# Experts of a two-layer AdaLN network: all tokens through all experts, or pairs sorted into 39 blocks

## The chip, the cores and the metric

The kernel runs on one core of one Trainium2 chip. The metric is the device time of one execution in microseconds. The core's engines are TensorE (PE, matrix products; PEld is its weight load), VectorE (DVE), ScalarE (ACT), GpSimd (POOL) and SyncE (SP, which issues transfers). Each runs its own program in order and waits for others by semaphores.

## What is computed

The reference has two layers; each adds a feed-forward result to `x` (8 sequences of 256 tokens, 512 channels). The first layer's condition is a chain of 256 oscillator steps, the second's is an attention with 16 heads. The change touches the last part only, the experts of the second layer:

```python
scores = einsum('btd,de->bte', x, router_w)
w, idx = top_k(softmax(scores), 2)
w = w / sum(w)
act = silu(x @ gate_proj[e]) * (x @ up_proj[e])     # 512 -> 256, for e in idx
out = sum over e in idx of w_e * (act @ down_proj[e])   # 256 -> 512
x = x + out
```

There are 2048 tokens, 8 experts and 2 chosen experts per token, so 4096 pairs of token and expert count; the reference is written over all 16384 and multiplies the others by zero.

## The kernel before

`build` runs three stages, each a block of its own: `oscillator_and_ffn`, `attention` and `experts`. The attention leaves its output y transposed in SBUF, channels on the partitions, as two 16-bit halves (`YH` the rounded value, `YL` the rest), and during it POOL prepares the gate and up weights of all experts as two halves in `WU`, scaled by 64. Every product is taken as high x high, high x low and low x high.

`experts` (from line 1187) first computes the router's scores with 192 small products (line 1294) into `dp[0]`; `route` on VectorE finds the two largest (lines 1346 and 1349), the two weights, and with 32 small operations (lines 1359 and 1360) a table `comb` of weights by token and expert. Meanwhile POOL scales and splits the down weights (lines 1245 to 1252).

Then the work runs over 4 groups of 512 tokens, and in a group over the 8 experts. For each expert and each half `fc` of its 256 hidden channels, `gate_up` (line 1270) takes 12 gate and 12 up products with the weights stationary and 512 tokens moving; ScalarE takes a tanh (line 1316), VectorE makes the hidden values and their two halves in four operations (lines 1368 to 1376). `down` (line 1284) takes 6 products for each of 4 tiles of 128 tokens, hidden values stationary, and VectorE's `fold` (line 1384) adds the result, times the token's weight for this expert, onto `acc`, which was loaded with the tokens of x (line 1233) and is stored at the end of the group (line 1236). TensorE's order per expert is: first half's gate and up, the previous expert's down, second half's gate and up.

Of the kernel before, what the change touches and what calls it, by code (L numbers as in the profile page):

```python
# [15 lines left out]
ALU = mybir.AluOpType  # L16
# [19 lines left out]
REP = 4  # L36

# [1142 lines left out]
def experts(nc, x1_dram, router, w_down, iota, WU, WD, YH, YL, out):  # L1180
    with ExitStack() as ctx:
# [6 lines left out]
        def psum(name):  # L1188
            return ctx.enter_context(nc.psum_tensor("moe_" + name, [P, 512], F32))

        TT = 4
        NG = B // 2
        NT = NG * TT
        dst = sb("dst", [P, HC, D])
        rst = sb("rst", [P, DC, E])
        rw = sb("rw", [P, 2, DC, E], F16)
        io = sb("io", [P, E])
# [8 lines left out]
        c1 = sb("c1", [P, NT, E])  # L1206
        comb = sb("comb", [P, NT * E])
        th = sb("th", [P, 2, 512])
        ga = sb("ga", [P, 512])
        hf = sb("hf", [P, 512])  # L1210
        hid = sb("hid", [P, FC, 2, 512], F16)
        acc = sb("acc", [P, TT, D])
        gp = [psum("gp0"), psum("gp1")]
        up = [psum("up0"), psum("up1")]
        dp = [psum(f"dp{i}") for i in range(TT)]
        FIRST = 2 * FC
        in_d = [sem("in_d0"), sem("in_d1")]
        in_r, d_scaled, d_hi, d_lo, r_hi, r_lo = (sem("in_r"), sem("d_scaled"), sem("d_hi"), sem("d_lo"), sem("r_hi"),
                                                  sem("r_lo"))
        sc_mm, dif_ok, ex_ok, comb_ok, own = sem("sc_mm"), sem("dif_ok"), sem("ex_ok"), sem("comb_ok"), sem("own_dve")  # L1220
        g_mm, u_mm, th_ok, hid_ok, d_mm, folded = sem("g_mm"), sem("u_mm"), sem("th_ok"), sem("hid_ok"), sem("d_mm"), sem("folded")
        acc_in, stored, ffn_own, halt = sem("acc_in"), sem("stored"), sem("ffn_own"), sem("halt3")
        block = ctx.enter_context(nc.Block())

        @block.sync
        def _(sp):
            sp.dma_start(rst[:], router).then_inc(in_r, 16)
            sp.dma_start(io[:], iota).then_inc(in_r, 16)
            sp.dma_start(dst[:, 0:FIRST], w_down[:, 0:FIRST]).then_inc(in_d[0], 16)
            sp.dma_start(dst[:, FIRST:HC], w_down[:, FIRST:HC]).then_inc(in_d[1], 16)  # L1230
            with sp.Fori(0, NG) as g:
                for tt in range(TT):
                    sp.dma_start(acc[:, tt], x1_dram[g * 2 + tt // 2][:, tt % 2]).then_inc(acc_in, 16)
                for tt in range(TT):
                    sp.wait_ge(folded, (g * E + E) * TT + tt + 1)
                    sp.dma_start(out[g * 2 + tt // 2][:, tt % 2], acc[:, tt]).then_inc(stored, 16)
                sp.wait_ge(stored, (g * TT + TT) * 16)
                sp.sem_inc(halt, 1)

        @block.gpsimd  # L1240
        def _(pool):
            def split_down(n):

                w = dst[:, bass.ds(n, 1)]
                pool.tensor_copy(WD[:, bass.ds(n, 1), 0], w).then_inc(d_hi, 1)
                pool.wait_ge(d_hi, n + 1)
                pool.sem_inc(halt, 1)
                pool.tensor_tensor(WD[:, bass.ds(n, 1), 1], w, WD[:, bass.ds(n, 1), 0], ALU.subtract).then_inc(d_lo, 1)

            for k, (first, last) in enumerate(((0, FIRST), (FIRST, HC))):  # L1250
                pool.wait_ge(in_d[k], 16)
                pool.tensor_scalar_mul(dst[:, first:last], dst[:, first:last], WS).then_inc(d_scaled, 1)
                pool.wait_ge(d_scaled, k + 1)
                pool.sem_inc(halt, 1)
                with pool.Fori(first, last) as n:
                    split_down(n)

        @block.tensor
        def _(pe):
            pe.wait_ge(r_lo, 1)  # L1260

            def gate_up(g, e, fc):

                n = (g * E + e) * FC + fc
                pe.wait_ge(hid_ok, n - FC + 1 + FC)
                for which, ps, done in ((0, gp[fc], g_mm), (1, up[fc], u_mm)):
                    k = 0
                    for wp, Yp in ((0, YH), (1, YH), (0, YL)):
                        for qt in range(DC):
                            last = pe.matmul(ps[:, :], WU[:, e * FC + fc, which, wp, qt, :],  # L1270
                                             Yp[:, bass.ds(g * 2, 2), qt, :], start=(k == 0), stop=(k == 3 * DC - 1))
                            k += 1
                    last.then_inc(done, 1)

            def down(g, e):
                pe.wait_ge(hid_ok, (g * E + e) * FC + FC + FC)
                pe.wait_ge(d_lo, e * FC + FC)
                for tt in range(TT):

                    pe.wait_ge(folded, (g * E + e) * TT + tt + 1)  # L1280
                    k = 0
                    for fc in range(FC):
                        for hp, wp in ((0, 0), (0, 1), (1, 0)):
                            last = pe.matmul(dp[tt][:, :], hid[:, fc, hp, tt * P:(tt + 1) * P], WD[:, e * FC + fc, wp, :],  # L1284
                                             start=(k == 0), stop=(k == 3 * FC - 1))
                            k += 1
                    last.then_inc(d_mm, 1)


            for tt in range(NT):  # L1290
                k = 0
                for wp, Yp in ((0, YH), (1, YH), (0, YL)):
                    for qt in range(DC):
                        last = pe.matmul(dp[0][:, tt * E:(tt + 1) * E], Yp[:, tt // 2, qt, (tt % 2) * P:(tt % 2 + 1) * P],  # L1294
                                         rw[:, wp, qt, :], start=(k == 0), stop=(k == 3 * DC - 1))
                        k += 1
            last.then_inc(sc_mm, 1)
            with pe.Fori(0, NG) as g:
                gate_up(g, 0, 0)
                gate_up(g, 0, 1)  # L1300
                with pe.Fori(1, E) as e:
                    gate_up(g, e, 0)
                    down(g, e - 1)
                    gate_up(g, e, 1)
                down(g, E - 1)

        @block.scalar
        def _(act):
            act.wait_ge(in_r, 32)
            act.activation(rw[:, 0].rearrange("p k e -> p (k e)"), rst[:].rearrange("p k e -> p (k e)"), ACT.Copy, scale=WS).then_inc(r_hi, 1)  # L1310

            def gate_tanh(g, e, fc):
                n = (g * E + e) * FC + fc
                act.wait_ge(g_mm, n + 1)
                act.wait_ge(hid_ok, n + 1)
                act.activation(th[:, fc], gp[fc][:, :], ACT.Tanh, scale=0.5 / WS).then_inc(th_ok, 1)
# [3 lines left out]
            with act.Fori(0, NG) as g:  # L1320
                with act.Fori(0, E) as e:
                    for fc in range(FC):
                        gate_tanh(g, e, fc)

        @block.vector
        def _(dve):
            dve.wait_ge(in_r, 32)
# [3 lines left out]
            dve.sem_inc(hid_ok, FC)  # L1331

            def route():

                k = [0]

                def step(ins):
                    ins.then_inc(own, 1)
                    k[0] += 1
                    dve.wait_ge(own, k[0])  # L1340

                dve.wait_ge(sc_mm, 1)
                step(dve.tensor_copy(sc[:].rearrange("p t e -> p (t e)"), dp[0][:, 0:NT * E]))
                dve.sem_inc(folded, TT)
                for tt in range(NT):
                    last = dve.max(top[:, tt], sc[:, tt])  # L1346
                step(last)
                for tt in range(NT):
                    last = dve.max_index(idx[:, tt], top[:, tt], sc[:, tt])  # L1349
                step(last)  # L1350
                dve.tensor_tensor(dif[:], top[:, :, 1], top[:, :, 0], ALU.subtract).then_inc(dif_ok, 1)
                step(dve.tensor_copy(idf[:], idx[:, :, 0:2]))
                dve.wait_ge(ex_ok, 1)

                step(dve.tensor_scalar(den[:], ex[:], WS, WS, ALU.mult, ALU.add))  # L1355
                step(dve.reciprocal(wt[:, 0], den[:]))
                step(dve.tensor_tensor(wt[:, 1], wt[:, 0], ex[:], ALU.mult))
                for tt in range(NT):
# [111 lines left out]
```

## Time and profile before

| | us |
|---|---|
| median of 3 runs | 3412.77 (3406.76 to 3414.52) |
| span of the profiled execution, first to last instruction | 3403.6 |
| its experts stage, from the attention's last slice to the end | 554.6 |

The runs lie 3 to 11 us above the span, which leaves out what happens ahead of the first and behind the last instruction; no time from outside is listed for the profiled execution itself. The profile gives for each engine the time in which it executes; TensorE's granted clock stands beside it in tenths or as a share of 2.4 GHz.

### The profile page before, as it was taken

The page shows a single profiled execution, that of the slowest core. Times are in us where ns is not written, and L with a number is a line of the kernel's source. Part 1 is how long each engine was busy: PE and PEld are TensorE (multiplying, and loading weights), DVE is VectorE, ACT ScalarE, POOL GpSimd, SP SyncE. Part 2 cuts the span into 40 slices and gives each one's busy share as a digit, 9 for nine tenths or more (in the row PEclk, how much of TensorE's full clock was granted, in tenths as well). Part 3 has the DMA queues.
Part 4 walks back from the last instruction along what each step waited for, and adds up shares of the span by engine and source line. Part 5 has one row for each costly group of instructions (what it writes and reads, how often), then busy time and mean ns, then how long its engine had stood idle before and what let it go on. Part 6 is the DMA issues. An engine that isn't in the chain of part 4 may idle for free. (4 is left out here: it accounts for less than half of the span.)

```text
span 3403.6 us, 128007 instructions
## 1 busy us (share of the span) xinstructions
PE 2702.1 (79%) x41104; PEld 1867.1 (55%) x41104; DVE 2621.4 (77%) x12682; ACT 1136.9 (33%) x3078; POOL 1361.7 (40%) x4206
## 2 busy tenths in 40 slices
PE   3377777777777777777777779988889995999999
PEld 2256566666555555555555546655556664444444
DVE  8888888888888888888888457788887877544444
ACT  2332222222222222222222247777776763000000
POOL 6745555555555555555555223323333325100000
PEclk9989988899999999999999875578885557999999
DMA  4100000000000000000000240111111011000000
GB/s 175 39 5 9 4 10 10 10 4 9 10 10 4 9 10 10 4 10 10 10 4 10 100 137 23 32 42 38 34 42 37 18 30 63 0 25 12 12 25 12
DMA packets 44052, 90.18 MB, mean 26 GB/s; under 512 B 7168, under 2 KB 23808, under 8 KB 41600
## 3 DMA queue, kind: packets, MB, share of 16 engines
q1 hardware_dynamic: 36336, 63.11, 5.8%
q10 hardware_dynamic: 4752, 10.49, 0.8%
q0 software_dynamic: 2304, 8.39, 0.8%
q8 instruction: 340, 5.57, 0.7%
q14 instruction: 320, 2.62, 0.3%
HBM read 65.18 MB, written 16.78 MB: 24 GB/s over the span
## 5 line engine op out<-in xcount | busy, mean ns | idle before, releaser
L225 PE MATMUL rest<-Tl,CW 128*128 128x32 f16 x16384 | 583.6, 179 | 489.6 <-DVE Tl L474 488.4
L225 PEld LDWEIGHTS rest<-Tl,CW 128*128 128x128 f16 x16384 | 489.8, 97 | 702.6 <-DVE Tl L474 693.5
L1060 PE MATMUL Tps<-idS,Pr 128*128 128x128 f32 x2048 | 425.7, 376 | 47.3 <-ACT Pr L1110 39.4
L1140 DVE CUSTOM_DVE_ANT_0 negL<-Lps,negC 128x512 f32<-128x512 f32 x512 | 342.2, 686 | 151.7 <-PE Lps L1050 134.8
L1060 PEld LDWEIGHTS Tps<-idS,Pr 128*128 128x128 f32 x2048 | 338.5, 194 | 164.4 <-DVE PT L1160 99.1
L644 POOL TENSOR_TENSOR G<-X,Dr 128x32 f32<-128x32 f32 x1024 | 268.6, 262 | 373.0 <-DVE X L479 299.0
L344 ACT ACTIVATE Tf<-X 128x32 f32<-128x32 f32 x768 | 176.1, 229 | 659.5 <-DVE X L554 658.2
L1117 ACT ACTIVATE PT<-Tps 128x512 f16<-128x512 f32 x512 | 300.1, 595 | 221.1 <-PE Tps L1060 220.5
L1110 ACT ACTIVATE Pr<-negL,nM 128x512 f32<-128x512 f32 x512 | 362.2, 720 | 20.3 <-DVE nM L1140 16.9
L1160 DVE TENSOR_TENSOR PT<-Tps,PT 128x512 f16<-128x512 f32 x512 | 348.2, 681 | 14.7 <-ACT PT L1117 10.0
L214 PE MATMUL main<-Th,CW 128*128 128x32 f16 x8224 | 250.9, 178 | 57.7 <-ACT Th L349 17.8
L1050 PE MATMUL Lps<-KR,QR 64*128 64x512 f16 x512 | 247.4, 519 | 42.1 <-issue 21.6
L214 PEld LDWEIGHTS main<-Th,CW 128*128 128x128 f16 x8224 | 225.0, 97 | 83.3 <-ACT Th L349 73.0
L648 POOL TENSOR_SCALAR gm<-X 128x32 f32<-128x32 f32 x768 | 233.7, 304 | 64.6
L1384 DVE SCALAR_TENSOR_TENSOR moe_acc<-moe_dp,moe_comb,moe_acc 128x512 f32<-128x512 f32 x128 | 96.1, 750 | 194.5 <-PE moe_dp L1284 194.5
L245 PE MATMUL gate<-Xa,WU 128*128 128x128 f16 x3072 | 236.3, 232 | 1.4 <-DVE Xa L562 1.4
L466 DVE TENSOR_TENSOR square<-X 128x32 f32<-128x32 f32 x1024 | 207.7, 203 | 32.6 <-DVE X L554 7.7
L245 PE MATMUL up<-Xa,WU 128*128 128x128 f16 x3072 | 229.9, 229 | 0.0
L1008 POOL TENSOR_TENSOR yf<-yn 128x64 f32<-128x64 f32 x128 | 40.9, 320 | 451.3 <-DVE yn L1154 451.3
L462 DVE SCALAR_TENSOR_TENSOR net<-main,G 128x32 f32<-128x32 f32 x768 | 142.7, 186 | 96.6 <-POOL G L644 90.8
L255 PE MATMUL acc_ps<-WD,hid 128*128 128x512 f16 x768 | 209.9, 382 | 0.6 <-ACT hid L358 0.6
L470 DVE SCALAR_TENSOR_TENSOR cube<-square,X 128x32 f32<-128x32 f32 x1024 | 204.3, 200 | 2.6 <-DVE lin L482 2.5
(135 smaller groups left out, 5056.4 us busy)
## 6 DMA issues: line engine op xcount, KB each, us to landing
stage<-w_up SPq DMA_DIRECT2D x8, 1024.0 KB, 4.8
qk<-qkp ACTq DMA_DIRECT2D x32, 256.0 KB, 2.4
QR<-qk SPq DMA_DIRECT2D x128, 64.0 KB, 2.2
KR<-qk SPq DMA_DIRECT2D x128, 64.0 KB, 2.4
wstage<-moe_up POOLq DMA_DIRECT2D x16, 512.0 KB, 6.3
W2m<-w_down SPq DMA_DIRECT2D x1, 4096.0 KB, 13.5
stage<-x_tb SPq DMA_DIRECT2D x16, 256.0 KB, 2.7
x<-stage SPq DMA_DIRECT2D x16, 256.0 KB, 2.6
```

The lines of the kernel that those rows point to most:

```text
L214: last = pe.matmul(main[:, m], CW[:, wp, k, m * P:(m + 1) * P], Th[:, par, k:k + 1, :].to_broadcast([P, REP, B]), start=(wp == 1 and m == ...
L225: last = pe.matmul(rest[:, m], CW[:, 0, k, m * P:(m + 1) * P], Tl[:, k:k + 1, :].to_broadcast([P, REP, B]), start=(m == 0 and k == 0), sto ...
L245: ins = pe.matmul(out[:, 0:P], WU[:, hc, which, wp, k, :], Xa[:, xp, k, :], start=(n == 0), stop=(n == 3 * DC - 1))
L255: ins = pe.matmul(acc_ps[:, :], hid[:, hp, :], WD[:, hc, wp, :], start=False, stop=False, skip_group_check=True)
L644: pool.tensor_tensor(G[:, s % 2, :], n, Dr[:, t, :], ALU.add).then_inc(drive_ready, 1)
L648: own.then_wait(pool.tensor_scalar_mul(gm[:], n, -EPS * a * BETA))
L1050: pe.matmul(Lps[qt % 2][:, :], QR[base:base + 64, h // 2, qt * P:(qt + 1) * P], KR[base:base + 64, h // 2, :], start=True, stop=True).then ...
L1060: last = pe.transpose(Tps[kc][:, qt * P:(qt + 1) * P], Pr[:, h % 2, qt, kc * P:(kc + 1) * P], idS[:])
L1110: act.activation(Pr[:, h % 2, qt, :], negL[:, qt, :], ACT.Exp, bias=nM[:, h % 4, qt:qt + 1], scale=-1.0).then_inc(s_exp, 1)
L1117: act.activation(PT[:, h % 2, 0, kc, :], Tps[kc][:, :], ACT.Copy).then_inc(s_hi, 1)
L1140: dve.tensor_tensor_reduce(out=negL[:, qt, :], in0=Lps[qt % 2][:, :], in1=negC[:], scale=1.0, scalar=3.0e38, op0=ALU.add, op1=ALU.min, acc ...
L1160: dve.tensor_tensor(PT[:, h % 2, 1, kc, :], Tps[kc][:, :], PT[:, h % 2, 0, kc, :], ALU.subtract).then_inc(s_lo, 1)
```

## The change

The pairs of token and expert are sorted on chip. Each expert has a region of 2048 + 128 rows in a buffer `xd` in device memory. A token tile's slot in the region comes from prefix sums over the one-hot mask (triangular and all-ones matrices in `moe_const`, products in `positions`). TensorE turns y back to tokens on the partitions (`token_rows`), ScalarE and four times VectorE copy it out as rows of 1024 16-bit values (high and low half), and POOL writes the rows with 32 indirect transfers, two for each of 16 tiles. SP pads each region's end with 128 zero rows, and 7 spare blocks. VectorE computes a table that gives, for each of 39 blocks of 128 rows (4096 / 128 + 7), the expert (`own_e`) and the first row (`own_r`).

The 39 blocks are written out one by one. For each, SP reads the row number out of SBUF into a register (`value_load`) and loads the block; TensorE turns it (8 transposes), takes 12 products with the tokens stationary and 512 columns of gate and up weights moving, turns the hidden values (4 transposes) and takes 6 down products; ScalarE copies the result out and SP stores it to `od`. At the end POOL gathers the two results of each token with 32 indirect transfers from `od` (into the space of `WU`), and VectorE adds them to x with the two weights. The split of the down weights is ScalarE's and VectorE's now. The buffers of the blocks lie in the space of `YH` and `YL`.

```diff
+            sp.wait_ge(padded, 16 * (E + SPARE))
+            sp.wait_ge(table_ok, 2)
+            sp.wait_ge(sent, 2 * NT * 16)
+
+            def load(i):
+                row = sp.value_load(own_r[0:1, i:i + 1], min_val=0, max_val=E * REGION + (SPARE - 1) * P)
+                if i >= NX:
+                    sp.wait_ge(t_mm, i - NX + 1)
+                sp.dma_start(xblk[:, i % NX], xd[bass.ds(row, P), :]).then_inc(x_in[i % NX], 16)
+
+            for i in range(NX - 1):
+                load(i)
+            sp.wait_ge(d_lo, HC)
+            for t in range(NT):
+                sp.dma_start(acc[:, t], x1_dram[t // 2][:, t % 2]).then_inc(acc_in, 16)
+            for i in range(NBLK):
+                if i + NX - 1 < NBLK:
+                    load(i + NX - 1)
+                sp.wait_ge(d_ok, i + 1)
+                sp.dma_start(od[i * P:(i + 1) * P, :], outs[:, i % NX]).then_inc(o_out[i % NX], 16)
+            for t in range(NT):
+                sp.wait_ge(sum2, t + 1)
+                sp.dma_start(out[t // 2][:, t % 2], acc[:, t]).then_inc(stored, 16)
...
         @block.gpsimd
         def _(pool):
...
+            pool.wait_ge(slot_ok, 1)
+            for t in range(NT):
+                wait_rows(pool, t)
+                for k in range(2):
+                    pool.indirect_dma_start(xd[:, :], bass.IndirectOffsetOnAxis(slot[:, k, t:t + 1], 0), rows[:, t], None).then_inc(sent, 16)
+            pool.wait_ge(home_ok, 1)
+            for n in range(NX):
+                pool.wait_ge(o_out[n], 16 * len(range(n, NBLK, NX)))
+            for t in range(NT):
+                for k in range(2):
+                    pool.indirect_dma_start(got[:, t, k], None, od[:, :],
+                                            bass.IndirectOffsetOnAxis(home[:, k, t:t + 1], 0)).then_inc(got_in[t // 2], 16)
...
         @block.tensor
         def _(pe):
...
+            def turn(i):
+                if i >= 2:
+                    pe.wait_ge(t_ok, i - 1)
+                pe.wait_ge(x_in[i % NX], 16 * (i // NX + 1))
+                for n in range(2 * DC):
+                    last = pe.transpose(tp[i % 2][:, n * P:(n + 1) * P], xblk[:, i % NX, n * P:(n + 1) * P], mats[:, 0])
+                last.then_inc(t_mm, 1)
+
+            def gate_up(i):
+                e = pe.value_load(own_e[0:1, i:i + 1], min_val=0, max_val=E - 1)
+                pe.wait_ge(t_ok, i + 1)
...
+                for q in range(DC):
+                    for xp, wp in ((0, 0), (0, 1), (1, 0)):
+                        last = pe.matmul(gu[i % 2][:, :, :, :], yt[:, i % 2, xp, q, :], WU[:, bass.ds(e * FC, FC), :, wp, q, :],
+                                         start=(n == 0), stop=(n == 3 * DC - 1))
...
+            turn(0)
+            turn(1)
+            e = gate_up(0)
+            pe.wait_ge(d_lo, HC)
+            for i in range(NBLK):
+                if i + 1 < NBLK:
+                    nxt = gate_up(i + 1)
+                turn_hidden(i)
+                if i + 2 < NBLK:
+                    turn(i + 2)
+                down(i, e)
+                e = nxt
...
         @block.scalar
         def _(act):
...
+            turned(0)
+            turned(1)
+            gate_tanh(0)
+            high(0)
+            for i in range(NBLK):
+                if i + 2 < NBLK:
+                    turned(i + 2)
+                if i + 1 < NBLK:
+                    gate_tanh(i + 1)
+                    high(i + 1)
+                out_copy(i)
...
         @block.vector
         def _(dve):
...
+            gated(0)
+            for i in range(NBLK):
+                hidden_turned(i)
+                if i + 1 < NBLK:
+                    gated(i + 1)
+            dve.wait_ge(acc_in, NT * 16)
+            for t in range(NT):
+                dve.wait_ge(got_in[t // 2], 16 * 4)
+                dve.scalar_tensor_tensor(acc[:, t], got[:, t, 0], wt[:, 0, t:t + 1], acc[:, t], ALU.mult, ALU.add).then_inc(sum1, 1)
+                dve.wait_ge(sum1, t + 1)
+                dve.scalar_tensor_tensor(acc[:, t], got[:, t, 1], wt[:, 1, t:t + 1], acc[:, t], ALU.mult, ALU.add).then_inc(sum2, 1)
```

Left out above: ScalarE's `turned` copies a turned block out of PSUM (128x1024), `gate_tanh` and `high` handle 128x256, `out_copy` copies the result of 128x512 and gives the signal `d_ok`. VectorE's `gated` makes the hidden values (two products of 128x256, then the low half), `hidden_turned` copies the turned hidden values out of PSUM.

## Rows read from the trace of the kernel before

**Rows 1.** Page, first line; timeline, POOL, end of the attention (start us, us).

```profile
span 3403.6 us, 128007 instructions
...
2848.71 0.30 POOL L1014 TENSOR_TENSOR YL<-yf,YH 128x64 f16<-128x64 f32 x1 [0.18 <-POOL YH L1011]
```

**Rows 2.** Busy time in the experts: stretch, us, engines (instructions), clock, DMA share, GB/s.

```profile
core 0: us, PE busy (x) PEld busy (x) DVE busy (x) ACT busy (x) POOL busy (x), PEclk, DMA share, GB/s
...
2898.00:3400.00 502.00, 493.17 (x2256) 221.57 (x2254) 247.11 (x379) 37.02 (x62) 11.75 (x13) 0.99 0.04 14
```

**Rows 3.** Page, part 4: the chain that ended last, shares by engine.

```profile
PE 15%; DVE 1%; issue 0%; DMA 0%; DVEq 0%; ACT 0%; SPq 0%
```

**Rows 4.** Timeline of the experts: two sweeps of down products; the last sum.

```profile
2967.40 5.34 PE L1284 MATMUL moe_dp<-WE,moe_hid 128*128 x24
...
2982.94 2.32 PE L1284 MATMUL moe_dp<-WE,moe_hid 128*128 x10
...
3400.20 0.75 DVE L1384 SCALAR_TENSOR_TENSOR moe_acc<-moe_dp,moe_comb,moe_acc 128x512 f32<-128x512 f32 x1 [0.54 <-PE moe_dp L1284]
```

**Rows 5.** Chain in order of time, way into the experts: start us, us, what.

```profile
2853.99 5.30 PE moe_dp L1294 x192
...
2860.97 2.28 DVE moe_idx L1349 x17
...
2865.56 0.29 DVE moe_c L1359
...
2893.02 0.65 DVE moe_comb L1362
...
2893.90 0.70 DVE moe_ga L1368
```

**Rows 6.** Timeline of the first layer: twelve products of 128 columns.

```profile
1501.52 0.83 PE L245 MATMUL gate<-Xa,WU 128*128 128x128 f16 x12
```

**Rows 7.** Timeline of the experts: products after a pause.

```profile
2897.59 3.59 PE L1270 MATMUL moe_gp<-YH,WU 128*128 x8 [26.71 <-DVE moe_hid L1376]
...
2902.65 1.89 PE L1270 MATMUL moe_up<-YH,WU 128*128 x8
...
3392.99 7.04 PE L1284 MATMUL moe_dp<-WE,moe_hid 128*128 128x512 f16 x24 [2.21 <-DVE moe_hid L1376]
```

**Rows 8.** Busy time in the attention, a stretch of 4 us (columns as rows 2).

```profile
2036.00:2040.00 4.00, 4.00 (x44) 2.79 (x43) 2.62 (x7) 3.62 (x7) 0.00 (x0) 0.50 0.03 6
```

**Rows 9.** Groups by shape, whole kernel: busy us, mean ns, idle before.

```profile
L1154 DVE TENSOR_TENSOR yn<-Ops,ri 128x128 f32<-128x128 f32 x128 | 35.9, 280 | 0.1
...
L869 DVE TENSOR_TENSOR V<-vp,V 128x256 f32 x32 | 12.1, 420 | 1.2 <-ACT V L831 0.3
L831 ACT ACTIVATE V<-vp 128x256 f32 x32 | 11.6, 390 | 2.7 <-PE vp L807 2.1
...
L436 DVE SCALAR_TENSOR_TENSOR WU<-stage,WU 128x512 f16<-128x512 f32 x32 | 21.8, 682 | 0.0
...
L825 ACT ACTIVATE qkp<-qp 128x512 f16<-128x512 f32 x16 | 8.8, 595 | 23.6 <-PE qp L798 19.5 <-issue 4.1
```

**Rows 10.** Instructions on tiles wstage and moe_acc: ns min/median/max, first, last start.

```profile
L984 POOL DMA_DIRECT2D wstage<-moe_up x16: 527/578/762, 2015.6 to 2740.7; - x16
L989 POOL TENSOR_SCALAR wstage<-wstage x16: 2765/2768/2770, 2042.7 to 2794.0; 128x1024 f32<-128x1024 f32 x16
...
L1233 SPq MOVE moe_acc<-x x16: 29/29/38, 2853.2 to 3276.9; - x16
L1233 SPq DMA_DIRECT2D moe_acc<-x x16: 332/346/570, 2853.2 to 3276.9; - x16
```

**Rows 11.** DMA view of 2851 to 2875, 40 slices of 0.6 us.

```profile
GB/s 0 3 29 167 55 341 410 437 587 410 655 246 410 601 205 492 492 287 532 492 174 331 304 403 413 256 55 38 7 0 0 0 0 0 0 0 0 0 0 0
DMA packets 1154, 5.30 MB, mean 221 GB/s; under 512 B 384, under 2 KB 384, under 8 KB 896
```

**Rows 12.** DMA issues of the kernel: count, KB each, median us to landing.

```profile
stage<-x_tb SPq DMA_DIRECT2D x16, 256.0 KB, 2.7
...
out<-moe_acc SPq DMA_DIRECT2D x16, 256.0 KB, 2.0
...
moe_rst<-router SPq DMA_DIRECT2D x1, 16.0 KB, 1.6
```

**Rows 13.** Waits of the whole kernel: us in total, times, longest us.

```profile
DVE X L457 <- issue: 39.1, 13, 3.3
```

More of the change, by code:

```diff
@@ L1177, in _, with experts @@
             all_heads(dve, step)
-def experts(nc, x1_dram, router, w_down, iota, WU, WD, YH, YL, out):
+def experts(nc, x1_dram, xd, od, router, w_down, const, WU, WE, YH, YL, out):
     with ExitStack() as ctx:
@@ L1220, in experts @@
[L1220 to L1223 removed]
+        oh = sb("oh", [P, 2, NT, E])
+        mask = sb("mask", [P, NT, E], F16)
+        place = sb("place", [P, NT, E])
@@ new lines, in experts @@
+        prod = sb("prod", [P, 2, NT, E])
+        slotf = sb("slotf", [P, 2, NT])
+        slot = sb("slot", [P, 2, NT], U32)
+        home = sb("home", [P, 2, NT], U32)
+        shift = sb("shift", [P, E])
+        cnt = sb("cnt", [P, E])
+        over = sb("over", [P, E, NT])
+        nb = sb("nb", [P, E])
+        part = sb("part", [P, E, E])
+        ends = sb("ends", [P, E])
+        past = sb("past", [P, NBLK, E])
+        gone = sb("gone", [P, NBLK, E])
+        who = sb("who", [P, NBLK])
@@ L1227, in _ @@
             sp.dma_start(rst[:], router).then_inc(in_r, 16)
[L1228 to L1238, printed above, removed]
+            sp.dma_start(cst[:], const).then_inc(in_c, 16)
@@ L1240, in _ @@
+            sp.wait_ge(stored, NT * 16)
         @block.gpsimd
         def _(pool):
[L1242 to L1246, printed above, removed]
-                pool.sem_inc(halt, 1)
[L1248 to L1256, printed above, removed]
+            pool.memset(blank[:], 0.0).then_inc(blank_ok, 1)
@@ L1275, in down @@
[L1275 to L1287, printed above, removed]
@@ L1296, in _, with token_rows @@
                         k += 1
             last.then_inc(sc_mm, 1)
[L1298 to L1305, printed above, removed]
+            pe.wait_ge(mats_ok, 1)
+            def token_rows(t):
+                if t >= 2:
+                    wait_rows(pe, t - 2)
+                for w, Yp in ((0, YH), (1, YL)):
+                    for q in range(DC):
+                        last = pe.transpose(tp[t % 2][:, (w * DC + q) * P:(w * DC + q + 1) * P],
+                                            Yp[:, t // 2, q, (t % 2) * P:(t % 2 + 1) * P], mats[:, 0])
+                last.then_inc(rows_mm, 1)
@@ new lines, in step, with flat @@
+            def step(ins):
+                ins.then_inc(own, 1)
+                k[0] += 1
+                dve.wait_ge(own, k[0])
+            def flat(x):
+                return x.rearrange("p t e -> p (t e)")
+            dve.wait_ge(in_c, 16)
+            dve.wait_ge(sc_mm, 1)
+            step(dve.tensor_copy(flat(sc[:]), rt[:, 0:P]))
+            for t in range(NT):
+                last = dve.max(top[:, t], sc[:, t])
+            step(last)
+            for t in range(NT):
+                last = dve.max_index(idx[:, t], top[:, t], sc[:, t])
@@ new lines, in _ @@
+            step(last)
+            step(dve.tensor_copy(idf[:], idx[:, :, 0:2]))
+            for w in range(2):
+                last = dve.tensor_tensor(oh[:, w], idf[:, :, w:w + 1].to_broadcast([P, NT, E]),
+                                         iota_e.unsqueeze(1).to_broadcast([P, NT, E]), ALU.is_equal)
+            step(last)
+            dve.tensor_tensor(mask[:], oh[:, 0], oh[:, 1], ALU.add).then_inc(mask_ok, 1)
+            dve.tensor_tensor(dif[:], top[:, :, 1], top[:, :, 0], ALU.subtract).then_inc(dif_ok, 1)
```

331 lines of the change are left out of this document (225 added, 106 removed).

## The prediction

> **What bounds the kernel now.** I read the page's parts 1 to 4 first, then the stretch of the experts alone, because that is the only stage that the change touches. The stage begins when POOL has written the last slice of the attention's output, at 2849.0 us, and ends with the span at 3403.6 [rows 1]: 554.6 us. In the stretch from 2898 to 3400, TensorE is busy 493 of 502 us at a granted clock of 0.99 (2.4 GHz), VectorE about half of it, ScalarE 7% and POOL 2% [rows 2]; the chain that ended last is TensorE's gate, up and down products [rows 3]. The timeline shows the pace: from one sweep of down products to the next are 15.54 us [rows 4], and a sweep (one expert, 512 tokens) has 72 products of 512 columns, so 0.216 us each. 32 sweeps are 497 us. The rest is the way in: scores at 2854, routing on VectorE until the first hidden block at 2893.9 [rows 5]. So here TensorE's columns are the bound, and most of them are wasted: every token goes through 8 experts and needs 2.
>
> **What the change removes.** 39 blocks of 18 products of 512 columns are 702 products instead of 2304. With 12 transposes a block TensorE has 18 x 0.216 + 12 x 0.06 = 4.6 us of work per block at the high clock (0.06 is the pace of the 128-column products [rows 6]). At the low clock a 512-column product takes 0.43 (eight in 3.59 us [rows 7]) and a block 18 x 0.43 + 12 x 0.11 = 9.0. That is 180 to 351 us. TensorE is no longer the natural bound; what comes in its place is a chain of waits, and I price that.
>
> **Way in.** Scores and the top-two search are as before, to 2863.2 [rows 5]. Then one-hot and mask, four operations of 128x128 at about 0.28 [rows 9]: 2864.4. Meanwhile TensorE turns eight token tiles and ScalarE copies them out, 128x1024 each. From 128x256 in 0.39 and 128x512 in 0.595 [rows 9] such a copy takes 0.595 + 512 x 0.0008 = 1.0 us; eight with hand-offs end near 2868.5. The prefix sums (32 small products) follow in TensorE's order, then five small VectorE operations: slots known at **2872**. The removed loop of 32 VectorE operations (2865.6 to 2893) pays for this part.
>
> **Scatter.** POOL now issues 32 indirect transfers, one after the other. The trace has no indirect transfer. The nearest row is POOL's plain one of 512 KB, 0.58 us of POOL [rows 10], and it computes no address per row; that is the lower end. Upwards I bound by four times that, 2.3, since each of 128 rows needs its index read and an address written; I take 1.1, twice the plain one. The Trainium skill (DMA: Bandwidth & Descriptors, Anatomy of one DMA) calls the cost of writing descriptors small; by it 0.58 would stand, data would bind, and the sum would be 16 us less. 32 x 1.1 = 35 us. The data is no harder limit: 8.4 MB plus 2.1 MB of padding at 0.35 MB/us (5.3 MB in 25 busy slices of 0.6 us [rows 11]) are 30 us. With a landing of 2.5 the last row is in memory at **2910**. Hidden beside it: the rest of the table, the other eight tiles, and the split of the down weights, moved from POOL to ScalarE and VectorE (16 x 0.6 and 16 x 0.68 us [rows 9], about 2888 to 2900). The data's 30 us cover them; without that cover they would cost at most 11.
>
> **First block.** SP looks up a row number in SBUF and loads block 0. The look-up (value_load) is not in the trace either. Lower end: a register MOVE, 0.03 [rows 10]; upper end: the shortest transfer, 1.6 [rows 12]. I take 1.0, nearer the upper end since it too must fetch from SBUF. The Trainium skill (DMA: Bandwidth & Descriptors, Latency and other measured facts) gives about 0.6 as the floor of such a load; by it each round below would be 0.4 shorter, the sum 14 us less. Then 0.48 to issue and 2.5 to land [rows 10, 12]. TensorE is at the low clock by then. Turn, copy, 12 products, hidden values, the products of block 1, and only then the turn of block 2, whose load stands on SP behind 16 issues of the x1 tiles (16 x 0.49 = 7.8): block 0's output is copied at about **2934**.
>
> **The rounds.** This is the term that decides. SP's order in the loop is: load block i+2, wait for block i's output, store it. So the load of block i+2 is queued behind the wait for block i-1's output (`d_ok`), and ScalarE's order is copy of turned block i+2, tanh of i+1, high half of i+1, output copy of i. Hence a closed chain from output i-1 to output i:
> - SP wakes 0.1, issues the store 0.48 (0.35 and a MOVE, with gaps [rows 10]), looks up the row 1.0, load to landing 2.5 (256 KB tiles took 2.0 to 2.7 [rows 12]; behind a store): 4.1.
> - TensorE sees it 0.15; eight transposes 1.0 at the low clock (12 products of 128 columns in 0.83 at the high one [rows 6]): 1.2.
> - ScalarE copies 128x1024, 1.0 + 0.1; tanh on 128x256, 0.39; VectorE's two products on 128x256, 0.42 each, with two hand-offs of 0.1; high half 0.4; output copy 128x512, 0.6 [rows 9]: 3.6.
>
> **8.9 us a block**, against 4.6 to 9.0 of TensorE work. From output 0 to output 36 are 36 rounds: 320 us, to 3254. The last two blocks have no load before them, about 7: **3261**. SP's wait holds loads and stores only; who waits for it is TensorE, and behind that everybody.
>
> **Way out.** Last store 2.5 with landing; POOL waits for all stores, then 32 indirect gathers x 1.1 = 35 (data alone 8.4 / 0.35 = 24), landing 2.5; the last pair of tiles needs four VectorE sums of 0.75, 3.0 [rows 4]; from the last sum to the span's end are 2.65 as before (3400.95 to 3403.6 [rows 1, 4]). Together 46: **3307**. Nothing overlaps here, the gather cannot begin before the last block is out.
>
> 3307 - 3403.6 = -96 us. The median of the runs, 3412.8, lies 9.2 above the profiled span; I keep that distance: **3316**. About 0.2%, 7 us, is what a measurement of this kernel can tell from no change.
>
> Priced at nothing: the unrolled code. The oscillator's loop shows 13 stalls of 3 us waiting for nothing visible, one per pass [rows 13]; straight code has no such jump. Were it to stall per block fetch, 10 of them would be 30 us.
>
> **Rivals.**
> *A short round.* If the look-up costs next to nothing and loads land in 2.0, a round is 7.4; with 0.58 per indirect transfer data binds, and 5 and 11 us more go. 36 x 1.5 = 54, with these 70: about **3246**. For it: the MOVE row. Against: a fetch from SBUF is no MOVE, and the store stands ahead of the load.
> *TensorE at the low clock binds.* The rows show the clock at 0.50 over stretches in which TensorE is busy 4.00 of 4.00 us [rows 8], and that a pause of 2.2 us before the last sweep was followed by 24 products in 7.04 us instead of 5.34 [rows 4, 7]. The chain leaves such pauses each round. If the whole round stays low, TensorE needs 9.0, plus its own look-up 1.0 and hand-offs: about 10 a round, +40: **3356**. The Trainium skill (TensorE: Matmul & The Clock Gate, Why this matters for your kernels) warns of idle gaps between bursts in just this way; the rows agree on the fall after a pause. Against: a round of nearly full work should raise the clock again, as after 2897.6 [rows 7].
> *Slower: POOL's indirect transfers.* All 64 stand alone on the path, 32 before the first block and 32 after the last. Break-even is 1.1 + 96/64 = 2.6 us each. At 3.4 the sum is +147: **3463**. For it: POOL's elementwise work is slow here, 2.77 us for 128x1024 [rows 10]. Against: the plain transfer's 0.58, with as many rows.
> That the change computes more than it says is excluded: the 39 blocks are fixed in the code.
>
> **How the numbers follow.** Forecast of 8.9 a round, 45%; TensorE low, 22%; short round, 18%; slower by the transfers, 15%. The predicted time is the likeliest's, 3316. Its unknowns: look-up 0.03 to 1.6 gives -35 to +22, landing 2.0 gives -18, indirect transfers -16 to +77. The low end is near the short round, 3245; the high end takes 2.3 per transfer and some of the low clock, 3425. Beyond lie about 8% below and 11% above. Faster than 3406: all of the first three cases but a few in 100, 0.83; within 0.2%, 0.03; slower, 0.14.
>
> **What would show it.** Right: TensorE's share in the block stretch falls to about half, blocks follow at 8 to 10 us, and the wait before the transposes of the loaded block goes to its DMA, whose issue follows the output copy. The first load stands near 2911, the first gather near 3264, and POOL's indirect rows show 1 us. Wrong: a round with TensorE waiting for VectorE or ScalarE only, loads landed long before; a granted clock near 0.5 with TensorE never idle; or a scatter and gather of over 80 us each.

## The result, and the profile after

The change made the kernel faster: 3302.09 us, median of 4 runs (3291.26 to 3307.5), against 3409.77 for the kernel before, median of 4 on the same chip (3390.31 to 3414.52). The ratio is 0.9667, with a 95% interval of 0.9618 to 0.9716. The prediction was 3316 (3245 to 3425). The profiled execution took 3306.22 us, its span is 3304.4. Three runs on the chip of the first experiments (3237.94 with a fourth load buffer, 3415.0 and 3429.08 of the kernel before) fell in a slower state of that chip and are left out of the ratios below.

First come the attention's end and the span, from the page's first line and from the tile `YL` (durations min/median/max in ns, first and last start in us), to be held against [rows 1]:

```profile
span 3304.4 us, 124760 instructions
L1021 POOL TENSOR_TENSOR YL<-yf,YH x128: 303/305/314, 2034.5 to 2875.6; 128x64 f32 x112, 128x64 f16<-128x64 f32 x16
```

The last slice of the attention's output is written at 2875.6 + 0.3 = 2875.9 us. So the experts' stage, which is all that the change touches, takes 3304.4 - 2875.9 = **428.5 us** where it took 554.6: 126 us less. The span shrank by 99 only, because the attention, whose code is the same, ended 26.9 us later here; the first experiment is about that.

The stage by stretches (start:end, length, then busy us and count of PE, PEld, DVE, ACT and POOL, the granted clock, the DMA share and GB/s), which answers to [rows 2]:

```profile
2898.00:2943.00 45.00, 4.74 (x40) 4.02 (x40) 17.58 (x39) 11.37 (x19) 32.88 (x32) 0.55 0.62 234
2943.00:2966.00 23.00, 15.42 (x69) 7.53 (x70) 2.96 (x7) 5.04 (x8) 0.00 (x0) 0.70 0.66 225
2966.00:3237.00 271.00, 191.35 (x1049) 93.32 (x1047) 59.20 (x140) 76.99 (x140) 0.00 (x0) 0.90 0.20 68
3237.00:3252.00 15.00, 9.50 (x56) 4.44 (x53) 3.71 (x9) 4.19 (x8) 0.00 (x0) 1.00 0.23 79
3252.00:3304.40 52.40, 0.00 (x0) 0.00 (x0) 23.35 (x32) 0.00 (x0) 32.65 (x32) 0.52 0.77 240
```

These are the scatter, the first block, the rounds, the last two blocks and the gather. TensorE had 493 of 502 us of work [rows 2]; in the rounds it has 191 of 271 (0.71), and the other engines less than a third. A stage bound by an engine has become one bound by a chain. The page's part 4 shows the same, with "DMA" in first place where [rows 3] had TensorE's products:

```profile
DMA 3%; issue 2%; POOL 2%; PE 2%; ACT 1%; DVE 1%; SPq 1%; POOLq 0%; ACTq 0%; DVEq 0%
```

The timeline of the kernel after, from one store to the next, shows the chain link by link (start us, duration us, engine, line, operation; in brackets the idle time before it and its releaser; TensorE's weight loads and other blocks' work are left out):

```profile
3096.11 0.33 SPq L1315 DMA_DIRECT2D od<-YH  x1
...
3097.20 0.34 SPq L1304 DMA_DIRECT2D YL<-xd  x1
...
3100.03 0.61 PE L1385 MATMUL moe_tp<-moe_mats,YL 128*128 128x128 f16 x8 [1.33 <-DMA YL<-xd]
...
3100.68 1.02 ACT L1468 ACTIVATE YL<-moe_tp 128x1024 f16<-128x1024 f16 x1 [4.59 <-PE moe_tp L1385]
3101.60 0.38 ACT L1474 ACTIVATE YH<-moe_gu 128x256 f32<-128x256 f32 x1
...
3102.01 0.42 DVE L1578 SCALAR_TENSOR_TENSOR YH<-YH,moe_gu 128x256 f32<-128x256 f32 x1 [2.84 <-ACT YH L1474]
3102.46 0.42 DVE L1583 SCALAR_TENSOR_TENSOR YH<-YH,moe_gu 128x256 f32<-128x256 f32 x1
3102.92 0.42 ACT L1480 ACTIVATE YH<-YH 128x256 f16<-128x256 f32 x1 [0.94 <-DVE YH L1583]
3103.24 0.58 ACT L1486 ACTIVATE YH<-moe_dp 128x512 f32<-128x512 f32 x1
...
3103.84 0.33 SPq L1315 DMA_DIRECT2D od<-YH  x1
```

Read it as a circle. The store of one block's output leaves SP's sequencer free, the load behind it is issued 1.09 us later, TensorE's transposes wait for its landing, ScalarE for the transposes, VectorE for the tanh, ScalarE again; and the output copy at the end, of the next block, is what SP's next store waits for: 3103.84 - 3096.11 = **7.73 us**. Over all the rounds with a load in them, the first store is issued at 2964.64 and the 37th at 3243.28: 278.6 / 36 = 7.74.

In the list of waits for the same stretch, 2966 to 3237 (total us, times, longest), the wait of ScalarE for the turned block is the largest, and the transposes wait for the load in every one of 35 rounds:

```profile
ACT YL L1468 <- PE moe_tp L1385: 161.2, 35, 5.2
...
PE moe_tp L1385 <- DMA YL<-xd: 79.7, 35, 3.4
```

The circle's last link is SP's own wait, the store for the output copy, in each of the 35:

```profile
SPq L1315 <- ACT YH L1486: 219.8, 35, 6.7
```

### The profile page after: what moved, and what is told of

It is laid out like the page before. It is cut to its first block and busy times, and to the rows that moved or that the text cites. A ratio compares the mean times of both kernels' runs of the same rounds, so it can differ in the third digit from the quotient of the medians.

```text
span 3304.4 us, 124760 instructions
## 1 busy us (share of the span) xinstructions
PE 2483.3 (75%) x40130; PEld 1791.2 (54%) x40130; DVE 2456.1 (74%) x12501; ACT 1212.4 (37%) x3199; POOL 1380.1 (42%) x4237
## 5 line engine op out<-in xcount | busy, mean ns | idle before, releaser
L1067 PE MATMUL Tps<-idS,Pr 128*128 128x128 f32 x2048 | 460.3, 397 | 25.0 <-ACT Pr L1117 22.0
L1067 PEld LDWEIGHTS Tps<-idS,Pr 128*128 128x128 f32 x2048 | 366.4, 206 | 156.9 <-DVE PT L1167 86.1
L1057 PE MATMUL Lps<-KR,QR 64*128 64x512 f16 x512 | 264.9, 560 | 39.9 <-issue 20.2
L351 ACT ACTIVATE Tf<-Cn 128x32 f32<-128x32 f32 x256 | 58.6, 229 | 390.4 <-DVE Cn L561 390.4
```

What stands on the lines that cost most here:

```text
L351: act.activation(Tf[:], src, ACT.Tanh).then_inc(tanh_full, 1)
L1057: pe.matmul(Lps[qt % 2][:, :], QR[base:base + 64, h // 2, qt * P:(qt + 1) * P], KR[base:base + 64, h // 2, :], start=True, stop=True).then ...
L1067: last = pe.transpose(Tps[kc][:, qt * P:(qt + 1) * P], Pr[:, h % 2, qt, kc * P:(kc + 1) * P], idS[:])
```

## Experiments

The stage is the time from the attention's last slice to the span's end, and a round the mean time between block stores from the first to the last (38 of them; for the kernel after this is 7.50, since the last two blocks have no load and take 3.2 each).

| kernel | attention ends, us | stage, us | round, us |
|---|---|---|---|
| before, shown profile and four more | 2849.0; 2864.5, 2866.5, 2876.4, 2841.3 | 554.6; 550.1, 550.2, 550.2, 550.1 | |
| after | 2875.9 | 428.5 | 7.50 |
| look-up four times | 2872.5 | 507.9 | 9.47 |
| a third of gate and up left out | 2857.5 | 429.2 | 7.54 |
| load one block earlier | 2905.4 | 330.8 | 4.88 |
| store on ScalarE's queue | 2859.6 | 329.0 | 4.90 |
| half the gathers | 2866.2 | 406.4 | 7.47 |
| x1 loads spread | 2857.3 | 421.3 | 7.52 |
| store on ScalarE's queue, x1 loads spread | 2873.7 | 322.9 | 4.85 |

### The kernel before again: is the later end of the attention the change's doing?

No edit; four more profiles of the kernel before.

> The kernel before, unchanged, once more: where does its attention end? In the profiled pair the attention ended at 2849.0 us before and at 2875.9 after the change, with the same code ahead of it. Theory: chance, the granted clock in the attention differs from one execution to the next; then the end here may lie anywhere between 2840 and 2880, and the end in the three kernels that follow scatters too. Rival: the change itself slows the attention by 27 us; then it ends at 2849 within 3 us here and near 2876 in the three that follow.

> A second profile of the unchanged kernel before, for the length of the attention alone. Theory (the attention's length varies from one execution to the next, whatever stands behind it): the attention's last slice ends anywhere in 2849 to 2905 us, as the profiles so far do. Rival (the change slows the attention by 15 to 27 us): with the kernel before it ends again at or below 2865.

> A third profile of the unchanged kernel before, with the same question. Theory: over these profiles the ends of the attention spread by 15 us or more and reach above 2866 at least once. Rival: all of them stay at or below 2865, and those with the change lie 10 us or more above on the mean.

> A fourth profile of the unchanged kernel before, with the same question and the same numbers as the third. The experts' stage behind the attention should again take 550 to 555 us, since nothing in it differs.

Measured: the attention ends at 2864.5, 2866.5, 2876.4 and 2841.3 us; with [rows 1] the same code has ended anywhere within 35 us. The windows of the attention's middle show what goes with it (columns as above): in the third of these profiles

```profile
2040.00:2840.00 800.00, 752.59 (x6233) 500.27 (x6232) 637.68 (x1675) 569.92 (x960) 246.09 (x480) 0.59 0.12 32
```

in the fourth

```profile
2040.00:2840.00 800.00, 722.03 (x6517) 487.21 (x6516) 658.60 (x1739) 583.70 (x994) 254.09 (x500) 0.69 0.12 32
```

and in the kernel after

```profile
2040.00:2840.00 800.00, 759.27 (x6187) 502.95 (x6185) 635.34 (x1667) 567.31 (x952) 245.74 (x479) 0.57 0.12 32
```

A granted clock of 0.69, 0.59, 0.57 goes with 6517, 6233 and 6187 products done in the same 800 us. The five profiles before end the attention at 2859.5 us in the mean, the eight with the change at 2871.0 (2857.3 to 2905.4): 11.5 apart, where either group scatters by more. So the 26.9 us are within what this code does from one execution to the next, and these profiles alone don't show a slowing by the change.

All runs together speak for one, however. The span of a run less the stage of its kernel (taken to be the same in each execution, 550.2 for the kernel before) gives an estimate of where its attention ended. Compared on one chip at a time, without the three runs left out above, the means are 2854 before and 2870 with the change (4 runs each), 2841 and 2862 (6 and 8), 2854 and 2863 (7 and 7): later by 15 us on the whole, with a 95% interval of about 5 to 26. Why the same code should end later there, and what makes the chip grant one or the other clock over the same instructions, was not found.

The stage is steadier by far: 550.1 to 550.2 in four profiles, 554.6 in the shown one. So the change gains 550.2 - 428.5 = 122 us in its stage, or 126 against the shown profile. The medians of the whole differ by 108 only; an attention that ends some 15 us later would be the difference. The ratio that 122 us would give, 1 - 122 / 3409.8 = 0.964, lies within the measured interval too.

### The closed chain: load one block further ahead

Theory: the load waits behind the store's wait on SP, so the round is the whole chain; rival: loads land late for want of bandwidth, or another engine paces. A fourth load buffer (NL is 4, NX stays 3) lets SP issue the load of block i+3 where it issued that of i+2 (the buffer's declaration and the index of the load are left out here):

```diff
+            load(NL - 2)
             for i in range(NBLK):
-                if i + NX - 1 < NBLK:
-                    load(i + NX - 1)
+                if i + NL - 1 < NBLK:
+                    load(i + NL - 1)
                 sp.wait_ge(d_ok, i + 1)
```

> A fourth load buffer, and each block's load issued one block earlier. Theory (the round is a closed chain: output copy, store, look-up, load, turn, copy, hidden values, output copy, 7.7 us): the load leaves the chain and a round falls to what is next, TensorE's 4.6 us of work at the high clock with hand-offs, so about 5.0; 36 x 2.7 = 97 us less than the changed kernel, about 3205. Rival (TensorE at a low clock sets the round): rounds stay above 7, time within 20 us of the changed kernel.

Measured: rounds of 4.88 us and a stage of 330.8, and a median of 3212.61 us over four runs (3174.68 to 3237.94; ratio to before 0.9436, 0.9313 to 0.9558). By the whole time this run and the next are rated unclear, with runs of the kernel before from 3359 to 3429 us beside them; the round and the stage decide. Same loads, same stores, same products; 98 us of the 428 were the place of the load in SP's order.

### The same from the other side: the store on another queue

SP only loads; ScalarE issues each block's store behind its own output copy.

```diff
-            for i in range(NBLK):
-                if i + NX - 1 < NBLK:
-                    load(i + NX - 1)
-                sp.wait_ge(d_ok, i + 1)
-                sp.dma_start(od[i * P:(i + 1) * P, :], outs[:, i % NX]).then_inc(o_out[i % NX], 16)
+            for i in range(NX - 1, NBLK):
+                load(i)
...
                 out_copy(i)
+                act.wait_ge(d_ok, i + 1)
+                act.dma_start(od[i * P:(i + 1) * P, :], outs[:, i % NX]).then_inc(o_out[i % NX], 16)
```

> Loads as far ahead as in the changed kernel, three buffers, but the stores of the blocks are issued by ScalarE behind its output copy, so that SP has loads only. Theory (SP's order, the load behind the store that waits for the output, closes the chain): the same gain by another way, rounds about 5.2 (ScalarE has 2.4 us of work and 0.4 for the issue), about 3215. If the length of the load matters and not its place behind the store: rounds stay above 7.

Measured: 4.90 us a round, a stage of 329.0, a median of 3186.67 us (0.9393, 0.9299 to 0.9487). Both cures give the same round to 0.02 us, so neither the fourth buffer nor the second queue as such is what helps. Here no load stands behind the wait for an output; with the fourth buffer a load still does, but it is one that is needed a round later, so that the circle has two rounds' time. The window and the chain of waits of this kernel (share of 2960 to 3120 by line) show what binds now:

```profile
2950.00:3130.00 180.00, 173.62 (x1093) 90.86 (x1090) 62.49 (x148) 80.30 (x147) 0.00 (x0) 1.00 0.31 102
...
by line: PE moe_gu L1393 52.8%; PE moe_dp L1415 30.2%; DVE YH L1593 9.0%; PE moe_hp L1405 4.9%; issue 3.2%
```

TensorE is busy 174 of 180 us at a clock of 1.00, and no transfer stands in the chain. 4.9 is near the 4.6 of TensorE's work that the prediction counted for a block at the high clock.

### TensorE's part in the round

The rival said that TensorE, at the low clock, paces the rounds. This kernel leaves out the gate and up products with the low half of the tokens, 4 of 12 a block, so its result is less exact.

```diff
-                    for xp, wp in ((0, 0), (0, 1), (1, 0)):
+                    for xp, wp in ((0, 0), (0, 1)):
...
-                                         start=(n == 0), stop=(n == 3 * DC - 1))
+                                         start=(n == 0), stop=(n == 2 * DC - 1))
```

> The changed kernel without the products of the low halves of the tokens with the gate and up weights (4 of 12 products a block are left out, so the hidden values are less exact). Judged by the rounds, from one block's store to the next, 7.7 us in the changed kernel, since the attention's end moves from run to run. Theory (closed chain through SP): the products stand in TensorE's time that is waited through anyway, so rounds stay at 7.6 to 7.8. Rival (TensorE sets the round): 4 x 0.22 to 0.43 = 0.9 to 1.7 us less a round, 6.0 to 6.8.

Measured: rounds of 7.54 and a stage of 429.2, against 7.50 and 428.5. A third of the largest term of TensorE's work is worth nothing; the transposes waited longer for the load instead, 91.4 us in the 32 rounds from 2970 to 3220 (2.9 each) where the kernel after shows 79.7 in 35 (2.3 each):

```profile
PE moe_tp L1385 <- DMA YL<-xd: 91.4, 32, 4.1
```

The rival falls. In the rounds of the kernel after the clock was 0.90 besides, not 0.50 (0.86 here).

### The price of a look-up

SP reads the row number four times instead of once ahead of every load.

```diff
-                row = sp.value_load(own_r[0:1, i:i + 1], min_val=0, max_val=E * REGION + (SPARE - 1) * P)
+                for _ in range(4):
+                    row = sp.value_load(own_r[0:1, i:i + 1], min_val=0, max_val=E * REGION + (SPARE - 1) * P)
```

> Each load looks its row number up four times instead of once; a look-up took 0.28 us of load and 0.17 of register work in the changed kernel. Theory (the look-up lies in the chain): 3 x 0.5 = 1.5 us more a round, 36 x 1.5 = 54 us, about 3356. Rival (TensorE sets the round): no difference, 3302 within 10.

Measured: a round of 9.47 against 7.50. Over the 36 rounds that have a load it is (3317.5 - 2965.1) / 36 = 9.79 against 7.74, 2.05 us more for three look-ups: **0.68 us each**. The stage is 79 us longer, where 54 had been written down. Two things follow. A look-up costs between the bounds of the prediction (0.03 and 1.6), less than the 1.0 taken there. And every part of it shows up in the end of the stage, as it must where SP's order lies on the chain. In the kernel after, one look-up consists of three visible pieces (ns min/median/max):

```profile
L1301 SPq TENSOR_LOAD <-moe_own_r x39: 274/278/537, 2942.5 to 3236.1; - x39
L1301 SPq FUSED_REGOPS  x39: 152/152/156, 2942.8 to 3236.4; - x39
L1301 SPq SEQ_ASSERT  x39: 18/18/18, 2943.0 to 3236.6; - x39
```

They sum to 0.45 us, and in the round shown above the look-up takes 0.57 with the gaps between them, by the chain in order of time (start us, us):

```profile
3096.49 0.28 SPq L1301
...
3096.80 0.15 SPq L1301
...
3097.06 0.04 SPq L1304
```

Part of the other 0.1 is that some of the loads take twice as long (up to 0.54 here, 0.55 in the kernel with four look-ups); the rest was not found. The Trainium skill (DMA: Bandwidth & Descriptors, Latency and other measured facts) gives about 0.6 as the floor of such a load; the 0.57 and 0.68 measured for a whole look-up lie on either side of it, and the prediction's own value was too high.

### The gathers at the end

16 of the 32 gathers are left out, each token's first expert row is added twice, so the second expert's result is missing.

```diff
-                for k in range(2):
+                for k in range(1):
...
-                dve.wait_ge(got_in[t // 2], 16 * 4)
+                dve.wait_ge(got_in[t // 2], 16 * 2)
...
-                dve.scalar_tensor_tensor(acc[:, t], got[:, t, 1], wt[:, 1, t:t + 1], acc[:, t], ALU.mult, ALU.add).then_inc(sum2, 1)
+                dve.scalar_tensor_tensor(acc[:, t], got[:, t, 0], wt[:, 1, t:t + 1], acc[:, t], ALU.mult, ALU.add).then_inc(sum2, 1)
```

> The changed kernel with 16 of the 32 gathers at the end left out (each token's second row is not fetched; its first is added twice). From the first gather to the end the changed kernel took 51.9 us. Theory (POOL issues the gathers one after another on the path, 0.96 us each and 0.30 between them): 16 x 1.26 = 20 us less, about 32. If the moving of the data were the bound, 4.2 MB less at 0.2 MB/us would also be 20 us, but then the transfers' landing times, 5.4 us for the last, should stay; if the way out hung on VectorE's 32 sums of 0.75 it would stay above 45.

Measured: from the first gather to the end 3272.6 - 3239.7 = 32.9 us, against 3304.4 - 3252.5 = 51.9: 19 us for 16 gathers, 1.19 each. The gathers are on the path one by one, as expected. Here is their row, and under it that of the kernel after:

```profile
L1337 POOL DMA_INDIRECT WU<-od,moe_home x16: 942/1142/1386, 3239.7 to 3260.4; - x16
```

```profile
L1337 POOL DMA_INDIRECT WU<-od,moe_home x32: 942/946/1444, 3252.5 to 3293.6; - x32
```

The saving is less than 16 x 1.33, the pace of the kernel after ((3293.64 - 3252.49) / 31). One reason is in the rows: the median gather took 1.14 us, not 0.95. VectorE's 32 sums, 24 us in all, are packed into the last part of this kernel, and set its end: from 3252.7 on they follow one another without a pause.

The rival that the moving of the data binds had a sign of its own, that the landing of the last gather stays: it did, at 5.6 us after its issue. The kernel after speaks against it even so. If data moved slower than POOL issues, each gather would land later than the one before it. Its gathers issued from 3252 to 3259, 3266 to 3280 and 3280 to 3294 land after these medians (us):

```profile
WU<-od,moe_home POOLq DMA_INDIRECT x6, 3.6
...
WU<-od,moe_home POOLq DMA_INDIRECT x11, 4.9
...
WU<-od,moe_home POOLq DMA_INDIRECT x12, 4.9
```

The landing grows at first, when the stores of the sums set in, and then no more, so the data keep up with POOL there. The margin is small: the DMA share is 0.77 in this stretch.

### The x1 loads

16 loads of x (one per tile, for the final sums) stand on SP between the loads of blocks 1 and 2. Here one of them follows each block's load instead.

```diff
-            for t in range(NT):
-                sp.dma_start(acc[:, t], x1_dram[t // 2][:, t % 2]).then_inc(acc_in, 16)
             for i in range(NBLK):
                 if i + NX - 1 < NBLK:
                     load(i + NX - 1)
+                if i < NT:
+                    sp.dma_start(acc[:, i], x1_dram[i // 2][:, i % 2]).then_inc(acc_in, 16)
```

> The 16 loads of x1 tiles go from ahead of the third block's load into the rounds, one a round, behind the block's load. Theory: the third block's load is issued 9 us earlier, at the end of which TensorE still works on the products of blocks 0 and 1, so the first store comes 4 us earlier (22 us after the first block's load is issued, where the changed kernel took 21.4 from 2943.2 to 2964.6: about 17.5), and the rounds stay at 7.6 to 7.9. Rival: the x1 loads, 0.7 us of data each, now lie beside the block loads and lengthen 16 rounds by up to 0.7: no gain or a loss of up to 7.

Measured: 14.9 us from the first load (2922.8) to the first store (2937.7), against 21.4 in the kernel after (2943.2 to 2964.6): 6.5 less, and the stage 7.2 shorter (421.3). The rounds stayed at 7.52, so a load of x behind a block's load costs them nothing. The gain is more than the 4 us expected. In the kernel after, the third block's load is not only issued late but also lands late, 6.33 us after its issue, behind the 16 loads; with these spread the same load landed in 3.3.

```profile
2953.96 6.33 DMA YL<-xd
```

### Both together

The store on ScalarE's queue and the x1 loads spread over the block loads (one behind each from block 2 on).

```diff
...
+            for i in range(NX - 1, NBLK):
+                load(i)
+                t = i - NX + 1
+                if t < NT:
+                    sp.dma_start(acc[:, t], x1_dram[t // 2][:, t % 2]).then_inc(acc_in, 16)
...
```

> Block stores on ScalarE's queue and the x1 loads spread over the rounds. Rounds 4.9 as with the stores on ScalarE alone; the stage from the attention's end to the end of the span 329 less about 4, 325 us; the time, with the attention ending anywhere between 2850 and 2905, near 3182.

Measured: the shortest stage, 322.9 us, with rounds of 4.85; the median is 3197.66 us, 16 above the time expected, and the ratio to before 0.9353 (0.9257 to 0.9449). Its interval overlaps with that of the store's move alone (0.9393), since the attention's end moves by more than the 6 us that the stage gained. By the stage, this is the best version: 227 us below the kernel before, 106 below the change as made.

## Why the prediction was right, point by point

Its steps, counted from the attention's end, against the kernel after:

| step | predicted, us | measured, us |
|---|---|---|
| slots known, first transfer of the scatter | +23 | +22.4 (2898.34) |
| last row in memory | +61 | +66.5 (2942.4) |
| first block's output stored | +85 | +88.7 (2964.64) |
| 36 rounds | 36 x 8.9 = 320 | 36 x 7.74 = 278.6 |
| last two blocks | 7 | 6.3 |
| way out | 46 | 54.8 |
| end | +458 | +428.5 |

**The mechanism** was right: the store's wait ahead of the next load closes a chain through all engines, and two runs that open it at different places bring the round down to 4.9, TensorE's own work. TensorE was no rival at 7.5 (a third of its gate and up left out changed nothing), and the indirect transfers, 1.31 to 1.33 us each, cost far from the 2.6 that would have eaten the gain. Of the signs named beforehand two did not come: TensorE's share in the rounds is 0.71, not about half, and a block takes 7.74 us, not 8 to 10. The second is the shorter round below; the first is that too, and TensorE's own work, 5.5 us a block (191 us in 35 rounds) where 4.6 to 9.0 was counted.

**The way in** came out at 22.4 instead of 23.

**The scatter** was undersized a little. The group of the 32 transfers (busy us, mean ns | idle before) reads

```profile
L1329 POOL DMA_INDIRECT xd<-moe_rows,moe_slot x32 | 32.9, 1027 | 28.7 <-DVE moe_slot L1540 19.3 <-issue 9.1 <-ACT moe_rows L1449 0.3
```

32.9 + 9.1 = 42 us, 1.31 each, where 1.1 was taken. A transfer itself is 1.03; what the prediction left out is the 0.30 between one and the next that waits for nothing visible. The Trainium skill (DMA: Bandwidth & Descriptors, Anatomy of one DMA) calls the cost of writing descriptors small, by which 0.58 would have stood; for this kind of transfer the measurement differs, 1.31 is more than twice the plain one [rows 10].

**The first block** took 22.2 us from the last row to its store, where 24 were predicted; the 16 x1 issues in it came to 8.4 us instead of 7.8, the load behind them landed in 6.3 instead of 2.5, and spreading them gave back 6.5. What made up for it in the 24 us can't be told, since the sum doesn't give the parts behind the load.

**The round** is the term that was mis-sized: 8.9 predicted, 7.74 measured, 41 us over 36 rounds. From store to load's issue the timeline has 1.09 us, where 0.48 for the store and 1.0 for the look-up were taken: 0.39 less, most of it the look-up, 0.57 in this round. From the load's issue to the transposes' start are 2.83 (landing and hand-off; 2.65 taken), the transposes 0.65 to the copy's start instead of 1.0, since the clock had not stayed low (0.90 in this stretch). From there to the store are 3.16 instead of 3.6: the tanh starts 0.10 before the listed end of the copy, the output copy 0.10 before that of the high half, and VectorE follows in 0.03. The hand-offs of 0.1 each and the 0.1 for SP's waking were counted on top, and mostly aren't there. So the round sits near the short round that the rival put at 7.4; there, though, the look-up was to cost next to nothing and loads to land in 2.0, and neither is so (0.57 to 0.68, and 2.6 in the median). One reading for the rival at the low clock was a little off: eight products in 3.59 us [rows 7] are 0.45 each, not 0.43, so a block's work at that clock is 9.4, not 9.0; that rival's round would have been as much longer, further from what came.

**The way out** was undersized by 9 us. The gathers stand 1.33 us apart, not 1.1: 41 from the first to the last against 35. And the last one ends late: it is issued at 3293.64, and the last pair's sums begin at 3299.01, behind a wait for it:

```profile
3293.64 0.95 POOL L1337 DMA_INDIRECT WU<-od,moe_home  x1 [0.30 <-issue]
...
3299.01 0.75 DVE L1604 SCALAR_TENSOR_TENSOR moe_dst<-WU,moe_wt,moe_dst 128x512 f32<-128x512 f32 x1 [3.19 <-DMA WU<-od,moe_home]
```

That is 5.4 from issue to use, where 2.5 was taken from plain loads.

**The total** came closer than its parts. The stage was 29.5 us shorter than predicted (428.5 against 458), and the attention 26.9 longer than in the profile that the sum was made against. And the distance kept between a span and the median, 9.2 us, was no overhead: the profiled execution after took 3306.22 at a span of 3304.4, so 1.8 lie around the span, and the other 7 of before were the attention's scatter. Together: 3316.2 - 29.5 + 26.9 - 7.4 = 3306.2. That the forecast of the total came within 14 us of the median is therefore luck: a longer attention, which it did not price, made up for most of a stage that was forecast 7% too long.

**At nothing** the prediction had the unrolled code's stalls, and the rounds show none: the chain's pace of 7.73 in one round equals the mean of 7.74, and the longest of the 36 took 8.37. The split of the down weights, moved to VectorE and ScalarE, lay beside the scatter as said; the slowest transfers, 1.50 us, stand in that stretch.

## What to carry to other kernels

On an engine that issues transfers in order, look at what each load is queued behind: a load that stands after a store's wait for an output ties the start of one block to the end of another, and all latencies in between add up, though no engine is busy all the time (0.71 for TensorE here, a third or less for the others). The cure is an order in which a load does not hang on the output of the block just ahead: a store on another queue, or one more buffer and each load a block earlier. Either was worth 98 to 100 us here, nearly as much as the change itself. When a stage's cost moves from an engine to a chain, sum the chain link by link, including the pieces of address look-up on the issuing engine, and compare stages and not whole runs where another stage scatters by more than the effect.

## What the runs showed of the hardware that was not expected

- The same attention code ended between 2841.3 and 2876.4 us in five profiles of the kernel before, with a granted clock of 0.69 to 0.59 in its middle. That is 1% of the kernel's time, without any change. By an estimate from all runs it ends some 15 us later with the change, for no cause that was found.
- An indirect transfer of 128 rows costs POOL 0.95 to 1.03 us plus 0.30 between two of them, and single ones 1.14 to 1.50 where VectorE was at work beside it (2909.9 to 2916.7 in the kernel after; most of the gathers where half are left out, 1.14 in the median). Whether VectorE's work is the cause was not tried apart.
- The last gather needed 5.4 us from its issue to the sum that uses it, twice the 2.6 of a plain 256 KB load.
- A register look-up from SBUF adds 0.57 to 0.68 us to a chain on SP, of which 0.45 are visible instructions.
